# Weights split on GpSimd during the causal attention, and two transformer layers run as one stream of chunks

## The reference

```python
xn = _layernorm(x, axis=-1)
s = _L0_attn_ref(xn, Wq, bq, Wk, bk, Wv, bv, Wo, bo)      # causal, 16 heads of 16
g = _silu(_L0_ffn_ref(xn, wqkv, q_scale, k_scale, wo, ln_g, ln_b, w1, b1, w2, b2))
x = x + s * g

def _layer(x, wqkv, qs, ksc, wo, lg, lb, w1, b1, w2, b2):  # twice, 8 heads of 64
    h = shift_token(x)                # second half of the columns one token later
    q, k, v = jnp.split(h @ wqkv, 3, axis=-1)
    q = l2norm(q) * qs; k = l2norm(k) * ksc
    q, k = rotary_xpos(q, k)
    o = local_attention(q, k, v)      # own window of 128 and the one before
    x = x + o @ wo
    h = shift_token(x)
    h = (h - mu) / jnp.sqrt(var + 1e-05) * lg + lb
    a, g = jnp.split(h @ w1 + b1, 2, axis=-1)
    return x + (a * gelu(g)) @ w2 + b2
```

## Time and profile before

| | us |
|---|---|
| median of three runs | 4926.27 |
| the profiled execution, its span from first to last instruction | 4929.3 |
| `prepare`, up to about | 200 |
| `attend`, up to its last output | 1879.3 |
| `layers`, layer 0, from its first load | 1882.7 |
| `layers`, layer 1, from its first load | 3339.6 |
| `combine`, from its first load | 4800.9 |

### The profile page before, as it was taken

One profiled execution on the slowest core, in us unless ns is written; L12 is line 12 of the kernel. 1 busy time (PEld: TensorE's weight loads), 2 busy tenths in 40 slices (PEclk: granted clock), 3 DMA queues, 4 the chain that ended last, 5 costly groups with the idle time before them and its releaser, 6 DMA issues. The chain is left out here.

```text
span 4929.3 us, 91933 instructions
## 1 busy us (share of the span) xinstructions
PE 4556.2 (92%) x32224; PEld 3000.4 (61%) x32224; DVE 3673.1 (75%) x7585; ACT 2989.0 (61%) x6873; POOL 1340.0 (27%) x1844
## 2 busy tenths in 40 slices
PE   8589999999999995999999999985999999999977
PEld 7434343343433433777777777764777777777757
DVE  7488888888888874777777777745777777777736
ACT  3167777777777773665656666642666666565632
POOL 3112111121112112433333333302333333333300
PEclk9789999999999997999999999997999999999988
DMA  8722422234222411000000000001000000000008
GB/s 300 218 34 41 59 40 37 36 47 56 37 37 36 57 18 66 10 14 14 14 10 15 13 14 14 14 5 65 10 14 14 14 14 14 14 14 10 14 13 273
DMA packets 174917, 214.21 MB, mean 43 GB/s; under 512 B 75068, under 2 KB 126228, under 8 KB 168340
## 3 DMA queue, kind: packets, MB, share of 16 engines
q1 hardware_dynamic: 174484, 208.56, 18.5%
HBM read 124.05 MB, written 83.89 MB: 42 GB/s over the span
## 5 line engine op out<-in xcount | busy, mean ns | idle before, releaser
L602 ACT ACTIVATE a_pt<-a_ring 128x512 f32<-128x512 f32 (+3 forms) x2560 | 1181.3, 544 | 414.8 <-PE a_ring L713 396.5
L653 DVE TENSOR_REDUCE a_mx<-a_ring 128x2 f32<-128x1024 f32 (+3 forms) x1092 | 1128.6, 1063 | 214.6 <-PE a_ring L733 114.4
L997 POOL TENSOR_TENSOR l_rn<-l_ssm,l_half 128x8 f32<-128x8 f32 x256 | 431.3, 1685 | 948.4 <-DVE l_ssm L1279 948.4
L726 PE MATMUL a_ring<-a_ks,a_qs 48*128 48x512 f32 (+3 forms) x2560 | 557.6, 431 | 91.0 <-DMA a_ks<-qk_d 57.4
L713 PE MATMUL a_ring<-a_qs,a_ks 49*128 49x512 f32 (+3 forms) x2560 | 559.5, 444 | 51.8 <-ACT a_pt L602 30.3
L750 PE MATMUL a_ot<-a_pt,a_vt 128*32 128x512 f32 (+3 forms) x5120 | 598.5, 547 | 1.8 <-ACT a_os L608 1.3
L713 PEld LDWEIGHTS a_ring<-a_qs,a_ks 49*128 49x128 f32 x2560 | 248.6, 187 | 455.5 <-ACT a_pt L602 272.6
L1098 ACT ACTIVATE l_pr<-l_pr,l_negm 128x256 f32<-128x256 f32 (+1 forms) x1024 | 500.6, 493 | 6.5 <-DVE l_negm L1331 6.1
L726 PEld LDWEIGHTS a_ring<-a_ks,a_qs 48*128 48x128 f32 x2560 | 259.1, 191 | 346.1 <-ACT a_pt L602 175.5
L576 POOL TENSOR_TENSOR a_gate<-a_gate 128x1 f32<-128x1 f32 x512 | 98.8, 193 | 1351.4 <-ACT a_pt L602 1341.4
L1004 POOL TENSOR_TENSOR l_work<-l_work,l_rot 128x512 f32<-128x512 f32 x256 | 357.1, 1396 | 395.2 <-DVE l_work L1287 395.2
(11 more groups left out here) (173 smaller groups left out, 9080.9 us busy)
## 6 DMA issues: line engine op xcount, KB each, us to landing
qk_d<-p_parts SPq DMA_DIRECT2D x16, 2048.0 KB, 10.9
a_qs<-qk_d SPq DMA_DIRECT2D x96, 256.0 KB, 8.2
a_ks<-qk_d SPq DMA_DIRECT2D x96, 256.0 KB, 18.6
x_d<-l_dx SPq DMA_DIRECT2D x32, 512.0 KB, 2.8
l_xt<-x_d SPq DMA_DIRECT2D x24, 513.0 KB, 3.7
p_x_in<-x SPq DMA_DIRECT2D x16, 512.0 KB, 8.8
x_d<-p_xt SPq DMA_DIRECT2D x16, 512.0 KB, 6.1
v_d<-p_vt SPq DMA_DIRECT2D x16, 512.0 KB, 11.8
```

The costliest lines, as they stand in the source:

```text
L602: act.activation(pt[:, (g * STEPS + s) % NPT, 2 * piece + f, q0:CHUNK], bank("step", g, k, f)[:, q0:CHUNK], ACT.Exp).then_inc(exp_done.sem, 1)
L653: r = dve.tensor_reduce(mx[:, pr, :, t, kc], ring[:, banks[0]:banks[1] + 1, 0:w], AX.X, ALU.max)
L726: mm = pe.matmul(bank("unit", G, n, f)[:, 0:w], qs[rows, v, pr, q0:q0 + P], ks[rows, v, pr, kc * CHUNK:kc * CHUNK + w], start=True, stop=k ...
L997: pool.tensor_tensor(out=rn[:, a * HEADS:(a + 1) * HEADS], in0=ssm[:, a * HEADS:(a + 1) * HEADS], in1=half[:, 0:HEADS], op=ALU.pow).then_i ...
```

## The change

1. `attend` gets weight work. `weight_items()` lists 16 items, eight a layer: two of wqkv, two of w1, one of wo, one of w2, two of the rotary tables. In group G SyncE brings item G in (`item_in`, after `row_out` 3), GpSimd splits it in pieces of 512 columns (`split`, after `widen`), and in the next group SyncE stores the high and low part to DRAM (`item_out`, after `out` 0). For w1 TensorE folds the shift into b1 (`fold`, 12 matmuls before step 47, in a bank of the ring) and VectorE adds it. In group 3 layer 0's wqkv is loaded into buffers that outlive the stage (`keep`).
2. `layers` has no `prepare_layer`. Its `program` is one loop over all 32 chunks. Layer 0's wqkv is there already; layer 1's is loaded in thirds when layer 0's last q, k and v projections are done (`wqkv`); wo, w1 and w2 of either layer are loaded split (`rest`).
3. The rotary table is no longer kept whole: each `fetch` brings the chunk's part, 512 KB, ahead of x.
4. All engines' orders in a chunk are written anew; the numbers of the events are shifted by whole chunks as well (`part_x1` of `c - 2` stands in round c instead of `c - 1`). The distance between a chunk's first projection and its `part_x1` stays two chunks.

The diff, cut to its core (the written orders are cut to TensorE's up to the first projections of a chunk):

```diff
+def weight_items():
+
+    return [(l, kind, k) for l in range(DEPTH)
+            for kind, n in (("wqkv", KT), ("w1", KT), ("wo", 1), ("w2", 1), ("rot", 2)) for k in range(n)]
...
-            do("step", 46); do("unit", 93); do("weigh", 18); do("step", 47); do("unit", 94); do("unit", 95)
+            do("step", 46); do("unit", 93); do("weigh", 18); do("fold", 0); do("step", 47); do("unit", 94); do("unit", 95)
...
+            def item_in(G, _):
+                l, kind, k = items[G]
+                if G == 0:
+                    sp.wait_ge(ones_in, 16 * 2 * NSLOT * NPAIR)
+                    sp.dma_start(scales[:, :, :], raw["scales"].partition_broadcast(P)).then_inc(small_in, 16)
+                    sp.dma_start(lng[:, :, :], raw["ln_g"]).then_inc(small_in, 16)
+                    sp.dma_start(lnb[:, :, :], raw["ln_b"]).then_inc(small_in, 16)
+                    sp.dma_start(b1raw[:, :, :], raw["b1"]).then_inc(small_in, 16)
+                    sp.dma_start(kept["b2"][:, :, :], raw["b2"]).then_inc(small_in, 16)
+                sp.wait_ge(lo_split.sem, lo_split.at(G - 1))
+                sp.wait_ge(parts_out.sem, parts_out.at(G - 1))
...
+            def item_out(G, _):
+                l, kind, k = items[G]
+                cols, rows = item_columns(kind), item_rows(kind)
+                sp.wait_ge(lo_split.sem, lo_split.at(G))
...
+            def keep(G, _):
+                if G != KEEP_AT:
+                    return
+                sp.wait_ge(parts_out.sem, parts_out.at(KT - 1))
+                for h, dst in enumerate((kept["wqkv_hi"], kept["wqkv_lo"])):
+                    sp.dma_start(dst[:, :, :].rearrange("p k n -> p (k n)").bitcast(F32), split_d["wqkv"][0, h])\
+                      .then_inc(kept_in, 16)
...
+                do("row_out", 1); do("row_out", 2); do("load", 1); do("out", -1); do("out", 0)
+                do("item_out", -1); do("row_out", 3); do("item_in", 0); do("row_out", 4); do("out", 1)
+                do("keep", 0); do("out", 2)
...
+            def split(G, _):
+                l, kind, k = items[G]
+                cols, rows = item_columns(kind), item_rows(kind)
+                pieces = [slice(a, min(a + CHUNK, cols)) for a in range(0, cols, CHUNK)]
+                if G == 0:
+                    pool.wait_ge(small_in, 16 * 5)
+                pool.wait_ge(raw_in.sem, raw_in.at(G))
+                if kind == "rot":
+                    for a in pieces:
+                        r = w_raw[:, a].rearrange("p (t n) -> p t n", n=4 * HD)
+                        op = pool.tensor_tensor(out=r, in0=r, in1=scales[:, l].unsqueeze(1)
+                                                .broadcast_to([P, CHUNK // (4 * HD), 4 * HD]), op=ALU.mult)
+                    op.then_inc(lo_split.sem, 1)
...
+                if kind == "w1":
+                    pool.wait_ge(folded.sem, folded.at(w1_items(G)))
+                    for a in pieces:
+                        op = pool.tensor_tensor(out=w_raw[:, a], in0=w_raw[:, a],
+                                                in1=lng[:, l, k:k + 1].broadcast_to([P, a.stop - a.start]), op=ALU.mult)
+                    op.then_inc(raw_scaled.sem, 1)
+                    pool.wait_ge(raw_scaled.sem, raw_scaled.at(l * KT + k))
+                pool.wait_ge(parts_out.sem, parts_out.at(G - 1))
+                for a in pieces:
+                    op = pool.tensor_copy(w_hi[0:rows, a], w_raw[0:rows, a])
+                op.then_inc(hi_split.sem, 1)
+                pool.wait_ge(hi_split.sem, hi_split.at(sum(i[1] != "rot" for i in items[:G])))
+                for a in pieces:
+                    op = pool.tensor_tensor(out=w_lo[0:rows, a], in0=w_raw[0:rows, a],
+                                            in1=w_hi[0:rows, a].bitcast(F32), op=ALU.subtract)
+                op.then_inc(lo_split.sem, 1)
...
+            def fold(G, _):
+                l, kind, k = items[G]
+                if kind != "w1":
+                    return
+                dve.wait_ge(folded.sem, folded.at(w1_items(G)))
+                if k:
+                    dve.wait_ge(b1_ready.sem, b1_ready.at(w1_items(G) - 1))
+                dve.tensor_tensor(out=kept["b1"][:, l], in0=bank("fold", G, 0)[0:MW, 0:2 * MT],
+                                  in1=kept["b1"][:, l] if k else b1raw[:, l], op=ALU.add).then_inc(b1_ready.sem, 1)
...
+            def fold(G, _):
+                l, kind, k = items[G]
+                if kind != "w1":
+                    return
+                pe.wait_ge(small_in, 16 * 5)
+                pe.wait_ge(raw_in.sem, raw_in.at(G))
+                wait_for_banks(pe, "fold", G, 0)
+                for m in range(2 * MT):
+                    mm = pe.matmul(bank("fold", G, 0)[0:MW, m:m + 1], w_raw[:, m * MW:(m + 1) * MW], lnb[:, l, k:k + 1],
+                                   start=True, stop=True)
+                mm.then_inc(folded.sem, 1)
...
-        def program(eng, prepare_layer, events, counts, around):
-
-
-            def part(l, b, first, end, more):
-                for c in range(first, end):
-                    def do(step, n):
-                        if n >= 0 and (more or n < counts[step]):
-                            d, n = divmod(n, counts[step])
-                            events[step](l * BATCH + (b + d), l, b + d, n, more)
-
-                    around(do, c)
-
-            for l in range(DEPTH):
-                prepare_layer(l)
-                part(l, 0, -2, 1, True)
-                for b in range(BATCH - 1):
-                    part(l, b, 1, CPB + 1, True)
-                part(l, BATCH - 1, 1, CPB + 1, False)
+        def program(eng, events, counts, around):
+
+
+            NB = DEPTH * BATCH
+
+            def do(step, n):
+                if 0 <= n < NB * counts[step]:
+                    B, n = divmod(n, counts[step])
+                    events[step](B, B // BATCH, B % BATCH, n, B < NB - 1)
+
+            for c in range(-4, NB * CPB + 6):
+                around(do, c)
...
+            def wqkv(B, l, b, n, more):
+                if l == 0 or b or n:
+                    return
+                for a, (name, per) in enumerate((("qk_done", -1), ("qk_done", 0), ("v_done", 0))):
+                    sp.wait_ge(S[name].sem, S[name].at(B, per))
+                    cols = slice(a * INNER, (a + 1) * INNER)
+                    for h, dst in enumerate((wqkv_hi, wqkv_lo)):
+                        sp.dma_start(dst[:, :, cols].bitcast(F32),
+                                     split_d["wqkv"][l, h].rearrange("p (k n) -> p k n", k=KT)[:, :, cols])\
+                          .then_inc(third_in[a], 16)
+
+            def rest(B, l, b, n, more):
+                if b or n:
+                    return
+                for name, hi, lo, rows, used in (("wo", wo_hi, wo_lo, P, ("wo_done",)),
+                                                 ("w1", w1_hi, w1_lo, P, ("g_done", "a_done")),
+                                                 ("w2", w2_hi, w2_lo, MW, ("w2m_done",))):
+                    for u in used:
+                        sp.wait_ge(S[u].sem, S[u].at(B, 0))
+                    for h, dst in enumerate((hi, lo)):
+                        sp.dma_start(dst[:, :, :].rearrange("p k n -> p (k n)").bitcast(F32), split_d[name][l, h, 0:rows])\
+                          .then_inc(rest_in[name].sem, 16)
 
             def fetch(B, l, b, c, more):
                 wait(sp, "x1_ready", B, (c - 1) * KT)
+                if l:
+                    sp.wait_ge(x_stored.sem, x_stored.at(B - BATCH, 16 * (c + 1)))
...
                 first = 0 if c else 1
+                sp.dma_start(rot[:, c % 2].rearrange("p t a d -> p (t a d)"),
+                             split_d["rot"][l, :, c * TPC * 4 * HD:(c + 1) * TPC * 4 * HD])\
+                  .then_inc(x_loaded[c % 2].sem, 16)
...
                 do("store", c - 1)
+                do("wqkv", c + 2)
+                do("rest", c)
                 do("fetch", c + 2)
...
+                do("turn_q", 4 * c - 3)
+                do("scores", 8 * c - 8)
+                do("turn_p", 16 * c - 18)
+                do("weigh", 16 * c - 20)
+                do("weigh", 16 * c - 19)
+                do("turn_k", 4 * c - 3)
+                do("turn_p", 16 * c - 17)
+                do("project", 8 * c - 1)
+                do("turn_d", 4 * c - 5)
+                do("weigh", 16 * c - 18)
+                do("weigh", 16 * c - 17)
+                do("scores", 8 * c - 7)
+                do("project_v", 4 * c - 2)
+                do("turn_p", 16 * c - 16)
+                do("part_x1", 2 * c - 4)
+                do("turn_q", 4 * c - 2)
+                do("turn_p", 16 * c - 15)
+                do("part_x1", 2 * c - 3)
+                do("turn_k", 4 * c - 2)
+                do("scores", 8 * c - 6)
+                do("mean", c - 2)
+                do("turn_p", 16 * c - 14)
+                do("weigh", 16 * c - 16)
+                do("weigh", 16 * c - 15)
```

(8 more changed lines are left out.)

666 lines of the change are left out of this document (319 added, 347 removed).

## The result

The changed kernel takes **4756.47 us**, the median of 4 runs (4743.15 to 4761.23), against 4927.52 for the kernel before; ratio 0.9641, 95% interval 0.9623 to 0.966. That is 171 us less. The forecast was 4805, with a range that began at 4780: the sign was right, the size fell short by 49 us. The profiled execution has a span of 4741.2 us and is the fastest of the four runs; a second profile of the same kernel (experiment e12) has 4755.9.

The account below looks back on a forecast made before the run. TensorE was taken to bound the layers' middles, order alone their ends. Span 4929.3 - 31 (front) - 102 (seam) + 12 (attention) + 0 (chunks) = 4808.3, so 4805 us as median; range 4780 to 4848 with the first two rivals.

Parts of the forecast that it names:

- first part: What bounds the kernel: TensorE full mid-layer, order at the ends; inside a chunk at most 26 us to win.
- part 4: Steady chunks with new order and rot load: no change, beat stays 84.4 us; loss bound +1.0 a chunk.
- bound of -0.5 us a chunk: Steady chunks: the most the rewritten order was allowed to gain; 0 was taken.
- Part 1, the front: Start of layer 0 without prepare_layer: first square 32.9 us sooner, booked as -31 us (28 to 35).
- the list of signs: Signs to look for, among them layer 0's first projection some 13 us after attention's last output.
- Part 2, the seam: Between layers 0 and 1: its cost goes except 7 us of wait for chunk 16's x; -102 us.
- The 108.8 us: Seam between the layers before: 362.0 us from fourteenth store to layer 1's first, against 253.2 at the beat.
- Part 3, attention: Attention stage: GpSimd's splits hidden, four folds of b1 not; +12 us (4 to 22).
- the port rule of the rival: Attention: GpSimd's splits take VectorE's time through a shared port, all 97 us on the path; 4902 us, chance 0.03.
- The slower one: Chunks: VectorE's rotates collide with GpSimd's cosines, two a chunk giving 141 us; 4946 us, chance 0.06.
- Small waits in each chunk: Steady chunks: the order rewritten for five engines adds 1.0 us of waits a chunk; 4837 us, chance 0.13.

Follow-up runs that it names:

- e12: The changed kernel run again unaltered, beside e11 on the same chip, to show one program's scatter; 4756.9 us.
- e1: Changed kernel with only TensorE's order altered: seven places with adjacent weigh events broken up by a neighbouring event; 4813.33 us.
- e3: Changed kernel with the old chunk orders of TensorE, VectorE, ScalarE and GpSimd; attention splits, joined stream and SyncE's new order stay; 4836.04 us.
- e11: Changed kernel with VectorE's fold sum earlier, fetch ahead of the wqkv thirds, and VectorE's layer semaphores opened before waiting for constants; 4723.91 us.
- e7: Changed kernel with SyncE's chunk order altered so that fetch goes ahead of the wqkv thirds; 4735.2 us.
- e4: Changed kernel without the fold's 12 matmuls and VectorE's addition; b1 copied in raw, the norm's shift left out; 4732.66 us.
- e5: Changed kernel with VectorE's part of the fold moved up from behind 16 reduces to behind 14; 4739.38 us.
- e8: Changed kernel with three exchanges of neighbours in TensorE's chunk order, for 27 tile-shape changes instead of 30; 4791.7 us.
- e10: Changed kernel with e11's edits, split parts sent ahead of attention outputs, and all sixteen weighs in eight pairs, two turn_p one event earlier; 4816.83 us.
- e2: Kernel before with only TensorE's order altered: seven pairs of weigh events put next to each other; 4926.14 us.

## Why the prediction was wrong

**The step that failed** is in its first part and in part 4: "a rewritten order therefore has almost nothing to win inside a chunk (32 x 0.8 = 26 us at the very most)", from PE's being busy 1095.10 of 1097.20 us and from the waits. The busy time was read rightly. The waits of the earlier trace rows are those of the weight loads (PEld), which run beside the matmuls; the matmuls themselves waited 1.8 us in those eleven chunks, so the margin was even smaller than taken. Neither bounds the gain. The bound of -0.5 us a chunk should have been at least -2.5: the order sets not only how long PE waits but how long it is busy, by the neighbours of each narrow matmul. e1 shows it for the new kernel (breaking seven pairs gives back 2.1 of the 2.5 us), e3 for the orders as a whole (back to 84.8). The other 0.4 to 0.6 us is the granted clock, of which the old orders lost more; e3 brings that back too, but which of its events does it no run shows. Over the three stages of chunks it made -71 us, of which the forecast had none.

The trace of before held it: the old order enters and leaves the narrow shapes 45 times a chunk, and starts of matmuls 0.203 apart stand beside starts 0.109 apart in it. The Trainium skill (TensorEngine Tiling (Array Packing), Key Properties) names a cause in words, that switching the tiling mode drains TensorE; it gives no price. The traces agree with it in so far as every change of shape costs time. By 15 changes at 0.094, read from the trace of before and the two orders, the forecast would have had -1.4 us a chunk, 45 us in all, and come to 4760. That this is nearly the measured median would have been luck: the chunks gave 26 us more than that, by the pairs' own gain and the clock, and attention and front took 16 more than forecast.

**Part 1, the front**: -26 against -31. The opening of the layers came 5.1 us behind the last output, as worked out. What was missed is that `fetch` waits for a semaphore that VectorE opens only once the constants have landed, so it was issued 4.3 us later than the opening and not 1. The first projection came 18.9 us behind the last output; the working has 15 (1894.4 less 1879.3), though the list of signs says 13. e11 takes the 3 us back at the projection, and not at the first store.

**Part 2, the seam**: right. The 108.8 us became 8.3 above three beats of 81.9, the forecast had 7, and the fetch did stand behind the v third (3187.11). e7 shows that it was the whole of the rest.

**Part 3, attention**: +23.4 in one profile and +29.6 in the other, against +12 (4 to 22). The splits are hidden as forecast; e4, which has them all, is 4.4 us over before, and the reduce's median, 1.216 us, is that of the earlier trace rows. So the port rule of the rival didn't bite here. The fold's passes (2.65) were sized well, the wait (8.5 us for all four, 6 forecast) a little low. The term left out was the granted clock: at each fold stood 10 us at half speed. Not all of that is new, since before had low clock elsewhere; from 400 us to the stage's last output it rose from 41 to 58 us, and half of that is 8.5. With the 2.5 of the waits this is the 11 us that the forecast lacks. e5 removes the waits and shortens the spells, and its stage pays 3.3 us; with 27 us of low clock, less than before had, a part of that is luck, and e11 pays 6.1.

**The rivals.** The slower one (rotates beside GpSimd's cosines) did not come: PE never waited for them, though single rotates took up to 1.56 us as before. Small waits in each chunk did not come either: PE waited 0.1 us a chunk. They were a real risk all the same, as e8 and e10 show with 1.2 and 2.4 us a chunk.

**Of the sum**: 4808 for the span, less 71 for the chunks, plus 11 for attention and 5 for the front, 6 for the combine stage and 6 for the seam's three faster beats off: 4741.

## What to carry over

An engine that is busy 99.8% of a stretch isn't at its floor: count how often TensorE's order changes tile shape, read the interval between starts at each change, and put events of one narrow shape side by side, provided the other engines' orders are moved with them: in e2, e8 and e10 events brought forward without their producers gave back as much as was won or more. Where one-column matmuls or a wait are added to TensorE, look at the granted clock right behind them and book that too.
